# Weight slabs loaded by one casting DMA from GpSimd, and attention without its two-stage order, in an eight-core transformer layer

## The reference

```python
x = x + layernorm(attn(layernorm(x), W_qkv, W_out, b_out))
x = x + layernorm(ffn(layernorm(x), w1, w2, w3))

def attn(x, W_qkv, W_out, b_out):          # attention is over the 16 heads of one token
    q, k, v = split((x @ W_qkv).reshape(b, s, 3, 16, 128))
    w = softmax(einsum('bshd,bsHd->bshH', q, k) / sqrt(128))
    return einsum('bshH,bsHd->bshd', w, v).reshape(b, s, 2048) @ W_out + b_out

def ffn(x, w1, w2, w3):                    # weights quantized to -1, 0, 1 by their mean size
    return bitlinear(sigmoid(bitlinear(x, w1)) * bitlinear(x, w2), w3)
def quantize(w): return clip(round(w / (mean(abs(w)) + 1e-8)), -1, 1)
```

## Time and profile before

| | |
|---|---|
| median of 4 runs | 4904.87 us (4889.35 to 5213.08) |
| profiled execution, its own time | 4905.42 us |
| its span, slowest of 8 cores | 4903.9 us |
| PE, DVE, ACT, POOL busy | 67%, 31%, 22%, 15% of the span |
| mean granted TensorE clock | 0.807 on that core |
| moved by DMA | 718.41 MB, mean 146 GB/s |

### The profile page before, as it was taken

The page is one execution under the profiler, slowest core; times in us unless marked ns, Lnnn a source line. Parts: engine busy times, 40 slices in busy tenths (PEclk is TensorE's granted clock), DMA queues, the critical chain, the costliest instruction groups (busy, mean ns, idle before and its releaser), DMA issues.

```text
span 4903.9 us, 46819 instructions; the slowest of 8 cores (4870.8 to 4903.9 us)
## 1 busy us (share of the span) xinstructions
PE 3274.7 (67%) x15948; PEld 1563.2 (32%) x15948; DVE 1511.4 (31%) x2623; ACT 1064.7 (22%) x1173; POOL 711.5 (15%) x1037
## 2 busy tenths in 40 slices
PE   2788611451599844473238888878975787887993
PEld 1333211220245433332113333333432333333441
DVE  3111122215667789855740000000022000000004
ACT  1666665441255522200000000000000000000000
POOL 1111111221144444433300000000000000000000
PEclk9978855675699855586568998989987899898996
DMA  8989744795488876669632122126443212212445
GB/s 139 266 249 269 243 157 155 226 302 157 138 257 265 247 205 200 203 195 199 193 104 69 52 53 67 52 60 115 92 125 107 69 52 63 58 52 68 94 88 154
DMA packets 734760, 718.41 MB, mean 146 GB/s; under 512 B 307776, under 2 KB 619200, under 8 KB 732352
## 3 DMA queue, kind: packets, MB, share of 16 engines
q0 software_dynamic: 120592, 438.37, 29.5%
q10 hardware_dynamic: 368768, 151.02, 12.8%
q1 hardware_dynamic: 245168, 126.03, 10.3%
HBM read 545.43 MB, written 157.29 MB: 143 GB/s over the span
## 4 chain that ended last, share of the span: by engine, by line
PE 49%; DMA 28%; DVE 11%; issue 7%; ACT 3%; ACTq 1%; SPq 0%; DVEq 0%; POOL 0%; POOLq 0%
PE pbig L1108 21%; PE pbig L1186 9%; DMA xstg<-w 9%; DMA wsf<-wqkv 9%; PE pscore L1108 6%; PE pbig L528 4%; PE pscore L1186 3%; PE pbig L714 3%; DVE stats L374 3%; DMA wsf<-w 3%; DMA bandw2b<-qw2T 2%; DMA bandw2a<-qw2T 2%; ACT xstg L839 1%; DVE xcst L945 1%; DVE xcst L950 1%
## 5 line engine op out<-in xcount | busy, mean ns | idle before, releaser
L528 PE MATMUL pbig<-t1f,wsb 128*128 128x512 bf16 x3072 | 731.1, 401 | 115.7 <-DVE wsb L484 112.0
L1186 PE MATMUL pbig<-hid,band 128*128 128x512 bf16 x2112 | 462.9, 382 | 22.8 <-DMA band<-qw3T 22.8
L528 PEld LDWEIGHTS pbig<-t1f,wsb 128*128 128x128 bf16 x3072 | 309.6, 102 | 516.1 <-issue 243.0
L1136 DVE TENSOR_TENSOR hid<-sigst,pbig 128x512 bf16<-128x512 bf16 x88 | 60.5, 688 | 1236.5 <-PE pbig L1108 1236.5
L1108 PE MATMUL pbig<-t1f,bandw1a 128*128 128x512 bf16 x1408 | 311.4, 382 | 168.1 <-DMA bandw1a<-qw1T 168.1
L1119 ACT ACTIVATE sigst<-pbig 128x512 bf16<-128x512 f32 x176 | 105.1, 597 | 1425.8 <-PE pbig L1108 1425.8
L1206 POOL DMA_DIRECT2D yscr<-ttok x64 | 34.6, 541 | 2201.8 <-issue 1647.3
L714 PE MATMUL pbig<-t1f,wsb 128*128 128x512 bf16 x1024 | 270.2, 430 | 89.3 <-DVE wsb L484 85.7
L1108 PE MATMUL pbig<-t1f,bandw1b 128*128 128x512 bf16 x1408 | 307.5, 379 | 0.0
L1108 PE MATMUL pbig<-t1f,bandw2a 128*128 128x512 bf16 x704 | 209.6, 465 | 135.6 <-DMA bandw2a<-qw2T 135.6
L1186 PEld LDWEIGHTS pbig<-hid,band 128*128 128x128 bf16 x2112 | 207.6, 98 | 275.8 <-issue 29.7
...
## 6 DMA issues: line engine op xcount, KB each, us to landing
xstg<-w POOLq DMA_DIRECT2D x294, 512.0 KB, 6.0
wsf<-w POOLq DMA_DIRECT2D x128, 512.0 KB, 5.8
wsf<-wqkv SPq DMA_DIRECT2D x192, 256.0 KB, 6.9
xcF<-w POOLq DMA_DIRECT2D x90, 512.0 KB, 6.2
band<-qw3T ACTq DMA_DIRECT2D x128, 352.0 KB, 5.9
wqkvb<-wsb POOLq DMA_DIRECT2D x48, 512.0 KB, 6.8
wsb<-wqkvb SPq DMA_DIRECT2D x48, 512.0 KB, 5.9
...
```

What stands on the lines that cost most here:

```text
L528: nc.tensor.matmul(p, w, r, start=st, stop=sp),
L1136: nc.vector.tensor_mul(d, a, p), inc="sV")
L1186: nc.tensor.matmul(p, w, r, start=st, stop=sp),
```

## The change

It has two parts.

In `_stream_wslab` both branches are replaced by one DMA from GpSimd. It reads the float32 slab from the weight tensor, casts on the way, and writes the bf16 buffer. GpSimd waits for the buffer to be free. The float32 staging, VectorE's casts and the bf16 scratch copies are gone, and chunk 1 reads float32 again. The callers are as they were, so the DMA is emitted before the slab's matmuls and after the jobs of the slab before.

In attention, the two-part order is replaced by one loop in which a step is emitted whole. The value transposes and their copy come right after the score matmuls, and `sexp`, `wdiv` and `sums4` have one buffer each.

```diff
 def _stream_wslab(b, ctx, chunk, wsrc, wbscr, m):
...
-    if chunk == 0:
...
-            qm = b.emit("sync", lambda e, d=dst, s=src: e.dma_start(out=d, in_=s),
-                        inc=f"dWf{q4 // 2}", inc_k=16)
...
-            m_c = b.emit("vector", lambda e, d=wsb[:, sl * D + hh * 1024: sl * D + (hh + 1) * 1024],
-                         s=wsf[:, hh * 1024:(hh + 1) * 1024]:
-                         nc.vector.tensor_copy(d, s), inc="sV")
...
-        m_st = b.emit("gpsimd", lambda e, d=wbscr[m, :, :], s=wsb[:, sl * D:(sl + 1) * D]:
-                      e.dma_start(out=d, in_=s), inc=f"{pref}{sl}", inc_k=16)
...
-    else:
...
-        m_l = b.emit("sync", lambda e, d=wsb[:, sl * D:(sl + 1) * D], s=wbscr[m, :, :]:
-                     e.dma_start(out=d, in_=s), inc=f"dWb{sl}", inc_k=16)
-        b.produced(wslab, m_l)
+    b.wait_free("gpsimd", wslab)
+    src = wsrc[:, m * 128:(m + 1) * 128].rearrange("(k p) c -> p k c", p=128)
+    dst = wsb[:, sl * D:(sl + 1) * D].rearrange("p (k c) -> p k c", c=128)
+    m_l = b.emit("gpsimd", lambda e, d=dst, s=src: e.dma_start(out=d, in_=s),
+                 inc=f"dWb{sl}", inc_k=16)
+    b.produced(wslab, m_l)
     return wslab, sl
...
-def _phase_attn_inner(b, ctx, chunk):
-    _attn_part1(b, ctx, chunk, 0)
-    for bt in range(1, NB):
-        _attn_part1(b, ctx, chunk, bt)
-        _attn_part2(b, ctx, chunk, bt - 1)
-    _attn_part2(b, ctx, chunk, NB - 1)
+def _phase_attn_inner(b, ctx, chunk):
...
+    for bt in range(NB):
+        pb = bt % 2
+        ps, sx, sm, wv, wt, vt = (("pscore", pb), ("sexp",), ("sums4",),
+                                  ("wdiv",), ("wtb",), ("vtb",))
...
+            b.wait_ready("vector", pv)
+            mev = b.emit("vector", lambda e, d=vtb[:, 0:512], s=ptx[0][:, 0:512]:
+                         nc.vector.tensor_copy(d, s), inc="sV")
...
+        b.wait_free("scalar", sx)
+        b.wait_ready("scalar", ps)
+        m_x = b.emit("scalar", lambda e, d=sexp[:, 0:512], s=pscore[pb][:]:
+                     nc.scalar.activation(d, s, AF.Exp), inc="sS")
...
```

More of the change, by code:

```diff
@@ L461, in _stream_wslab @@
     nc = b.nc
-    wsf, wsb = ctx["wsf"], ctx["wsb"]
+    wsb = ctx["wsb"]
     sl = m % 2
     wslab = ("wsb", sl)
-    if chunk == 0:
[L466 to L473, removed]
-            qm = b.emit("sync", lambda e, d=dst, s=src: e.dma_start(out=d, in_=s),
-                        inc=f"dWf{q4 // 2}", inc_k=16)
[L476 to L481, removed]
-            m_c = b.emit("vector", lambda e, d=wsb[:, sl * D + hh * 1024: sl * D + (hh + 1) * 1024],
-                         s=wsf[:, hh * 1024:(hh + 1) * 1024]:
-                         nc.vector.tensor_copy(d, s), inc="sV")
[L485 to L488, removed]
-        m_st = b.emit("gpsimd", lambda e, d=wbscr[m, :, :], s=wsb[:, sl * D:(sl + 1) * D]:
-                      e.dma_start(out=d, in_=s), inc=f"{pref}{sl}", inc_k=16)
[L491 to L494, removed]
-    else:
-        b.wait_free("sync", wslab)
-        b.wait_ready("sync", "wst_done_" + wbscr.name[:4] + "_0")
-        b.wait_ready("sync", "wst_done_" + wbscr.name[:4] + "_1")
-        m_l = b.emit("sync", lambda e, d=wsb[:, sl * D:(sl + 1) * D], s=wbscr[m, :, :]:
-                     e.dma_start(out=d, in_=s), inc=f"dWb{sl}", inc_k=16)
-        b.produced(wslab, m_l)
@@ L549, in _phase_qkv @@
         b.produced(n, mark)
-def _attn_part1(b, ctx, chunk, bt):
+def _phase_attn_inner(b, ctx, chunk):
     nc = b.nc
[L554 to L606, removed]
@@ L609, in _attn_part2 @@
[L609 to L612, removed]
-    atf = t1f
[L614 to L679, removed]
@@ L682, in _phase_attn_inner @@
-def _phase_attn_inner(b, ctx, chunk):
-    _attn_part1(b, ctx, chunk, 0)
-    for bt in range(1, NB):
-        _attn_part1(b, ctx, chunk, bt)
-        _attn_part2(b, ctx, chunk, bt - 1)
-    _attn_part2(b, ctx, chunk, NB - 1)
+    (qg, kg, vg, pscore, pmix, sexp, sums4, wdiv, wtb, vtb,
+     ident, mask01, t1f) = (ctx[k] for k in (
+        "qg", "kg", "vg", "pscore", "pmix", "sexp", "sums4",
+        "wdiv", "wtb", "vtb", "ident", "mask01", "t1f"))
+    atf = t1f
+    b.wait_ready("tensor", "qkvg")
@@ new lines, in _phase_attn_inner @@
+    b.wait_ready("tensor", "consts")
+    last_sc = last_tv = last_mx = None
+    for bt in range(NB):
+        pb = bt % 2
+        ps, sx, sm, wv, wt, vt = (("pscore", pb), ("sexp",), ("sums4",),
+                                  ("wdiv",), ("wtb",), ("vtb",))
+        b.wait_free("tensor", ps)
+        mm = None
+        for g4 in range(4):
+            gi = bt * 4 + g4
+            mm = b.emit("tensor", lambda e, p=pscore[pb][:, g4 * 128:(g4 + 1) * 128],
+                        q=qg[:, gi * 128:(gi + 1) * 128], k=kg[:, gi * 128:(gi + 1) * 128]:
+                        nc.tensor.matmul(p, q, k, start=True, stop=True),
+                        inc="sT" if g4 == 3 else None)
+        b.produced(ps, mm)
+        last_sc = mm
+        if ATTN_PARTS < 2:
+            b.consumed(ps, mm)
+            continue
+        if ATTN_PARTS != 15:
+            b.wait_free("tensor", vt)
+        mev = None
+        ptx = ctx["ptx"]
+        if ATTN_PARTS != 15:
+            pv = ("ptbank", 0)
+            b.wait_free("tensor", pv)
+            mtv = None
+            for g4 in range(4):
+                gi = bt * 4 + g4
+                mtv = b.emit("tensor", lambda e, p=ptx[0][:, g4 * 128:(g4 + 1) * 128],
+                             s=vg[:, gi * 128:(gi + 1) * 128], idn=ident[:]:
+                             nc.tensor.transpose(p, s, idn),
+                             inc="sT" if g4 == 3 else None)
+            b.produced(pv, mtv)
+            last_tv = mtv
+            b.wait_ready("vector", pv)
+            mev = b.emit("vector", lambda e, d=vtb[:, 0:512], s=ptx[0][:, 0:512]:
+                         nc.vector.tensor_copy(d, s), inc="sV")
+            b.consumed(pv, mev)
+        if mev is not None:
+            b.produced(vt, mev)
+        if ATTN_PARTS == 12:
+            b.consumed(ps, mm)
+            continue
+        b.wait_free("scalar", sx)
+        b.wait_ready("scalar", ps)
+        m_x = b.emit("scalar", lambda e, d=sexp[:, 0:512], s=pscore[pb][:]:
+                     nc.scalar.activation(d, s, AF.Exp), inc="sS")
+        b.consumed(ps, m_x)
+        b.produced(sx, m_x)
+        b.wait_free("vector", wv)
+        b.wait_ready("vector", sx)
+        b.wait_ready("vector", "consts")
+        m_mm = b.emit("vector", lambda e, d=wdiv[:, 0:512], s=sexp[:, 0:512], mk=mask01[:]:
+                      nc.vector.tensor_mul(d, s, mk), inc="sV")
+        b.consumed(sx, m_mm)
+        b.produced(wv, m_mm)
+        b.wait_free("vector", sm)
+        b.wait("vector", "sV", m_mm[1])
+        m_s = b.emit("vector", lambda e, d=sums4[:, 0:4],
+                     s=wdiv[:, 0:512].rearrange("p (g x) -> p g x", g=4):
+                     nc.vector.tensor_reduce(d, s, AX.X, ALU.add), inc="sV")
+        b.wait("vector", "sV", m_s[1])
+        m_r = b.emit("vector", lambda e, d=sums4[:, 4:8], s=sums4[:, 0:4]:
+                     nc.vector.reciprocal(d, s), inc="sV")
+        b.produced(sm, m_r)
+        b.wait_free("vector", sx)
+        m_d = None
+        for g4 in range(4):
+            b.wait("vector", "sV", m_r[1])
+            m_d = b.emit("vector", lambda e, d=sexp[:, g4 * 128:(g4 + 1) * 128],
+                         s=wdiv[:, g4 * 128:(g4 + 1) * 128],
+                         r=sums4[:, 4 + g4:5 + g4]:
+                         nc.vector.tensor_scalar(d, s, r, None, ALU.mult), inc="sV")
+        b.produced(sx, m_d)
+        b.consumed(wv, m_d)
+        b.consumed(sm, m_d)
+        if ATTN_PARTS < 3:
+            continue
+        b.wait_free("tensor", wt)
+        pw = ("ptbank", 1)
+        b.wait_free("tensor", pw)
+        b.wait_ready("tensor", sx)
+        mtw = None
+        for g4 in range(4):
+            mtw = b.emit("tensor", lambda e, p=ptx[1][:, g4 * 128:(g4 + 1) * 128],
+                         s=sexp[:, g4 * 128:(g4 + 1) * 128], idn=ident[:]:
+                         nc.tensor.transpose(p, s, idn),
+                         inc="sT" if g4 == 3 else None)
+        b.produced(pw, mtw)
+        b.consumed(sx, mtw)
+        b.wait_ready("vector", pw)
+        mew = b.emit("vector", lambda e, d=wtb[:, 0:512], s=ptx[1][:, 0:512]:
+                     nc.vector.tensor_copy(d, s), inc="sV")
+        b.consumed(pw, mew)
+        b.produced(wt, mew)
+        if ATTN_PARTS < 4:
+            continue
+        b.wait_free("tensor", ("pmix",))
+        b.wait_ready("tensor", wt)
+        b.wait_ready("tensor", vt)
+        mmx = None
+        for g4 in range(4):
+            mmx = b.emit("tensor", lambda e, p=pmix[:, g4 * 128:(g4 + 1) * 128],
+                         v=vtb[:, g4 * 128:(g4 + 1) * 128],
+                         w=wtb[:, g4 * 128:(g4 + 1) * 128]:
+                         nc.tensor.matmul(p, v, w, start=True, stop=True),
+                         inc="sT" if g4 == 3 else None)
```

(23 more changed lines are left out.)

## The result

The changed kernel took 6206.38 us, the median of 7 runs, against 4919.24 us for the one before on the same chips. The ratio is 1.267, with a 95% interval of 1.262 to 1.273: 27% slower. Some executions of every kernel here take some per cent longer, with the cores of one die at a lower granted clock; the ratios, and times not called a median, leave them out. The profiled execution has a span of 6201.2 us, 1297 more than before, and a mean granted TensorE clock of 0.756 on that core, where it was 0.807.

The account below looks back on a forecast made before the run. Each stage had its own bound: DMA bytes, dependent instructions, TensorE or VectorE. Terms 726 + 231 + 200 - 30 + 19 + 30 = +1176 on 4905.4 us gave 6081, stated as 6080 us, range 5850 to 6400.

Parts of the forecast that it names:

- QKV 0 and its start: First-chunk QKV: later first matmuls, then 9.6 us per slab against 10.5; -30 us, bounds -85 and +60.
- attention 0: First-chunk attention: losing the software pipeline adds 0.6 us to each of 32 steps, +19 us.
- projection 0: First-chunk output projection: slab load queued behind the result's store and six job loads; 427 against 227 us, +200.
- QKV 1: Second-chunk QKV: nothing prefetched, 13.7 us wait plus 9.8 us matmuls per slab; 1114 against 388 us, +726.
- attention 1 and projection 1: Second chunk: VectorE idles during transposes in attention, +30 us; projection waits 16.4 us per slab, +231 us.
- norms, the remaining jobs, FFN: Parts given no growth in the sum, norms lying between first projection and second QKV; FFN unchanged at 2377 us.
- The order of GpSimd's list: GpSimd runs its list in order, so second-chunk slab loads issue only after the previous slab's matmuls and jobs; +726 in QKV.
- a ring: First-chunk attention: closed chain from one exponential to the next, 9.88 us per step, growing to 10.5.
- Its first step: First-chunk QKV: load of slab m+1 issues 4.5 us after the matmuls of m-1, through ScalarE's job.
- The landing: Time from a slab load's issue to its arrival, taken as 7.5 us; forecast covers 5.5 to 10.
- 77 serial waits: Unhidden slab waits: 47 in second-chunk QKV, 15 in each projection; 77 us for each microsecond of landing.

Follow-up runs that it names:

- one_ahead: The changed kernel with each slab load emitted one slab earlier, ahead of the previous slab's matmuls and jobs; median 5256.63 us, ratio 1.064.
- two_ahead: The changed kernel with the load of slab m+2 emitted right behind slab m's matmuls, ahead of m's jobs; median 5122.01 us, ratio 1.036.
- plain_same_place: The kernel before, with only the second chunk's plain bf16 slab load moved to GpSimd, at the changed kernel's place; two runs, 5887 and 5935 us.
- attn_only: The kernel before with the new attention loop and its old slab loads; median 4997.34 us, ratio 1.010.
- cast_later: The changed kernel with the 8 MB cast of x moved behind the first chunk's QKV; lowest of three runs 6234 us.
- long_rows: two_ahead with the slab read in 8 KB rows instead of 512-byte pieces, so it does not compute the layer; one run, 5005.01 us.

## Why the prediction was right

It said 6080 (5850 to 6400), the median is 6206. The profiled spans show in which stage the error lies. Predicted and measured growth by stage, in us:

| | predicted | measured | |
|---|---|---|---|
| QKV 0 and its start | -30 | +76 | ends at 671.3 instead of 595.8 |
| attention 0 | +19 | +24 | |
| projection 0 | +200 | +189 | |
| QKV 1 | +726 | +753 | |
| attention 1 and projection 1 | +261 | +265 | 820 instead of 555 |
| norms, the remaining jobs, FFN | 0 | -9 | |
| sum | +1176 | +1297 | |

**The order of GpSimd's list** was the right mechanism: shown by one_ahead and two_ahead, which change nothing else, and by plain_same_place, which has the loss without a cast. In QKV 1 the load stands 6.3 us after the matmuls (predicted 6.1), 15.0 us pass until the next ones start (13.7), and these take 8.9 (9.8), the first ones at the lower clock level: two errors that nearly cancel, 23.9 us per slab against 23.5. That the stage came out so close is in part luck.

**Projection 0** went as laid out from the earlier trace rows. The changed kernel, one slab:

```profile
1099.66 3.83 PE L686 MATMUL pbig<-t1f,wsb 128*128 128x512 bf16 x17
...
1105.23 0.56 POOL L703 DMA_DIRECT2D yscr<-qg  x1 [17.28 <-DVE qg L696]
...
1115.52 0.54 POOL L806 DMA_DIRECT2D xstg<-w  x1 [0.73 <-ACT xstg L811]
1116.09 1.16 POOL L468 DMA_DIRECT2D wsb<-wout  x1
...
1125.33 8.72 PE L686 MATMUL pbig<-t1f,wsb 128*128 128x512 bf16 x32 [21.83 <-DMA wsb<-wout]
```

The slab is issued 12.6 us after the matmuls' end at 1103.49 (predicted 12.0) and lands at 21.8 (19.5), one of the later ones: over the twelve steps with jobs the wait is 20.2 us, and 9.4 in the three after them (9.7). The matmuls are a microsecond faster.

**Attention 0** is a ring still, now 818.82 - 808.33 = 10.49 us where 10.5 was predicted, against 9.88 in the earlier trace rows:

```profile
808.33 0.58 ACT L576 ACTIVATE sexp<-pscore 128x512 bf16<-128x512 f32 x1
...
812.20 0.43 DVE L622 COPY wtb<-ptb 128x512 bf16<-128x512 bf16 x1 [0.83 <-PE ptb L616]
...
818.82 0.58 ACT L576 ACTIVATE sexp<-pscore 128x512 bf16<-128x512 f32 x1
```

In attn_only the second attention stage grew by 30, as predicted (by some 35 on the other cores, inside the prediction's bounds).

**QKV 0** is the term that was wrong, in sign, by 106 us of the 121 by which the sum is short. Its first step was right: the load of slab m+1 hangs on ScalarE's job of m-1.

```profile
309.83 15.48 PE L497 MATMUL pbig<-t1f,wsb 128*128 128x512 bf16 x64 [6.12 <-DMA wsb<-wqkv]
...
318.50 2.34 ACT L508 ACTIVATE kg<-pbig 128x512 bf16<-128x512 f32 x1 [1.12 <-PE pbig L497]
...
322.96 1.16 POOL L468 DMA_DIRECT2D wsb<-wqkv  x1
...
331.62 16.52 PE L497 MATMUL pbig<-t1f,wsb 128*128 128x512 bf16 x64 [6.31 <-DMA wsb<-wqkv]
```

It is issued 322.96 - 318.50 = 4.5 us after the evacuation of that slab starts, exactly as reckoned from the earlier trace rows. But it lands after 8.7 us instead of 7.5, and TensorE takes its idle time in one piece of 6.3 us per two slabs rather than about 2.5 per slab; behind it the first matmuls run at the lower clock level, and the first slab takes 8.7 us instead of 7.1. The rows before held a warning: PE busy 389 us for 48 slabs is 8.1 us per slab, not 7.1. Two slabs take 331.62 - 309.83 = 21.8 us instead of 19.1: 2.7 us for each of the 23.5 pairs, 64 us. The first matmuls start at 115 us and the second slab at about 123, not 112: the first slab's load waits 53 us at most behind the cast of x. That is 11 more. The last 30 us are landings of up to 12 us in parts of the stage (the mean is 11.6 us per slab, not 10.9); the cast of x is not what makes them late (cast_later), and pieces of 512 bytes have a part in it: long_rows lands in 6.1 us where two_ahead needs 9.6 in this stage. The rest was not separated. The wrong conclusion was that 20% fewer bytes would let this stage gain: its DMA share fell from 0.87 to 0.73, so bytes stopped being its bound. Nor did the DMA engines gain a fifth: 0.87 x 506 = 440 us of their time became 0.73 x 556 = 406, 8% less. one_ahead, at 465 us, shows that they could have been worth some 40 us with the load in a better place.

**The landing** was taken at 7.5 us from issue; the medians by line show it longer in the changed kernel.

```profile
wsb<-wqkv POOLq DMA_DIRECT2D x96, 512.0 KB, 8.6
...
wsb<-wout POOLq DMA_DIRECT2D x32, 512.0 KB, 8.1
```

By stage it is 8.6 us in QKV 1 and in projection 1, and 7.7 in projection 0. Over the 77 serial waits that is about 70 us more than predicted. But it does not explain why the measured time lies above the forecast: in the three rows of the table with these waits the sum is only 27 - 11 + 4 = 20 us short, because the shorter matmuls gave back 0.9 x 48 = 43 us in QKV 1 alone. What lies above the forecast is QKV 0. The range held because the large terms, the serial ones, were right.
